# A graph layer with a mixture of experts: experts scatter finished rows to the output by node number

## The reference

```
logits = h @ gate_w + gate_b                      # h = layernorm(x), 3125 x 256; 8 experts
idx, prb = argmax(softmax(logits)), max(softmax(logits))
pos = rank of the token among those of its expert; kept = pos < C      # C = 489
buf[idx, pos] = h                                 # 8 x 489 x 256, empty slots are 0
ybuf = relu(buf @ w1 + b1) @ w2 + b2              # w1 256 x 1024, w2 1024 x 256 per expert
y = nan_to_num(ybuf[idx, pos] * (prb * kept), nan=0, posinf=1e4, neginf=-1e4)
out = x + y
```

## Time and profile before

| what | us |
|---|---|
| median of three runs | 1727.82 (1725.07 to 1732.25) |
| the profiled execution's own time | 1727.49 |
| its span | 1725.8 |
| TensorE busy | 1058.0 (61%) |
| VectorE busy | 972.2 (56%) |
| GpSimd busy | 538.4 (31%) |
| ScalarE busy | 432.9 (25%) |

### The profile page before, as it was taken

One profiled execution on the slowest core, in us unless ns is written; L12 is line 12 of the kernel. 1 busy time (PEld: TensorE's weight loads), 2 busy tenths in 40 slices (PEclk: granted clock), 3 DMA queues, 4 the chain that ended last, 5 costly groups with the idle time before them and its releaser, 6 DMA issues. The chain is left out here.

```text
span 1725.8 us, 20777 instructions
## 1 busy us (share of the span) xinstructions
PE 1058.0 (61%) x4059; PEld 687.7 (40%) x4060; DVE 972.2 (56%) x2394; ACT 432.9 (25%) x1253; POOL 538.4 (31%) x608
## 2 busy tenths in 40 slices
PE   0489483655666556565656655565668709999950
PEld 0255251433343333343334333343335605666630
DVE  5479865667666666667666666666777400000016
ACT  1222251322222222222222222222232402212111
POOL 1234425333334344343333444333300060000024
PEclk9999765777677677668776777667789558999985
DMA  4622404443444444444334444444300231323214
GB/s 142 112 92 65 125 14 122 117 119 111 112 124 125 115 133 130 121 124 122 111 111 122 130 131 131 125 117 129 99 1 0 73 107 51 126 94 128 87 39 122
DMA packets 86446, 179.36 MB, mean 104 GB/s; under 512 B 14979, under 2 KB 51909, under 8 KB 86413
## 3 DMA queue, kind: packets, MB, share of 16 engines
q0 software_dynamic: 39872, 117.67, 24.9%
q1 hardware_dynamic: 42125, 57.30, 10.5%
q10 hardware_dynamic: 4416, 4.01, 0.7%
HBM read 157.65 MB, written 21.63 MB: 104 GB/s over the span
## 5 line engine op out<-in xcount | busy, mean ns | idle before, releaser
L1099 PE MATMUL at_pa<-at_pv,at_hot 128*125 128x264 f32 x832 | 321.5, 532 | 229.3 <-DVE agg L973 160.3
L1099 PEld LDWEIGHTS at_pa<-at_pv,at_hot 128*125 128x125 f32 x832 | 193.3, 253 | 329.5 <-issue 256.9
L1042 PE MATMUL at_pq<-q,at_hotT 125*128 x1248 | 232.7, 330 | 79.5 <-DVE at_prod L981 56.9
L845 POOL DMA_INDIRECT slot<-kv_d,idx x192 | 183.5, 956 | 294.9 <-ACT idx L854 239.7
L845 POOL DMA_INDIRECT at_slot<-kv_d,idx x192 | 183.4, 955 | 289.7 <-ACT idx L854 236.9
L1042 PEld LDWEIGHTS at_pq<-q,at_hotT 125*128 125x128 bf16 x1248 | 142.5, 114 | 165.4 <-issue 112.0
L973 DVE TENSOR_TENSOR agg<-agg,at_pa 125x264 f32 x416 | 176.4, 424 | 33.5 <-remote 6.8
L1436 DVE TENSOR_TENSOR yb<-xp,b 128x256 f32<-128x256 f32 (+1 forms) x32 | 13.6, 425 | 269.5 <-PE xp L1467 269.5
L1016 DVE TENSOR_TENSOR at_pv<-at_slot,at_pp 128x528 f32<-128x528 f32 x104 | 71.8, 700 | 125.0 <-remote 91.8
L1016 DVE TENSOR_TENSOR at_pv<-slot,at_pp 128x528 f32<-128x528 f32 x104 | 71.7, 700 | 121.4 <-remote 87.0
L902 DVE TENSOR_REDUCE at_sc<-at_prod 128x16 f32<-128x512 f32 x208 | 139.2, 670 | 0.0
(11 more groups left out here) (295 smaller groups left out, 1408.4 us busy)
## 6 DMA issues: line engine op xcount, KB each, us to landing
slot<-in_w SPq DMA_DIRECT2D x16, 1024.0 KB, 7.5
at_locrow<-loc_d SPq DMA_DIRECT2D x26, 500.0 KB
slots_d<-slot SPq DMA_DIRECT2D x7, 512.0 KB
kv_d<-vst SPq DMA_DIRECT2D x25, 128.9 KB
base<-in_x SPq DMA_DIRECT2D x5, 625.0 KB
kv_d<-kst SPq DMA_DIRECT2D x25, 125.0 KB
slot<-kv_d,idx POOLq DMA_INDIRECT x192
at_slot<-kv_d,idx POOLq DMA_INDIRECT x192
```

Source lines behind the costliest of these rows:

```text
L845: pool.indirect_dma_start(slot[par][:, u, :], None, m.kv_d, bass.IndirectOffsetOnAxis(ap=m.idx[:, par, u:u + 1].bitcast(U32), axis=0)).the ...
L1042: mm = pe.matmul(pq[j % 2][:, (u % 2) * D:(u % 2 + 1) * D], hotT[:, u, :], at(m.q3, window)[:, part, :], start=(part == 0), stop=(part == 2))
L1099: mm = pe.matmul(pa[u % 4][:, 0:H * VW], hot[:, u % 8, :], pv[:, u % 4, :, :].rearrange("p h c -> p (h c)"), start=True, stop=True)
```

## The change

Each slot row gets two more columns (RW = 258): the token's probability (PRB) and its node number as an integer (NODE). The tile of h that is scattered, `m.hx`, has them beside h; empty slots have a node number beyond all nodes, written when the slot rows are zeroed. `attention_out` stores the residual twice while it is made, in five groups of five tiles each: to `x2_d` in DRAM and to `out`, both by SyncE. In `experts`, GpSimd gathers the residual of the rows of expert e+1 from `x2_d` by the node numbers that came with the rows (`xb`), VectorE scales, does the nan_to_num and adds the residual for each tile of 128 rows (eight operations), and GpSimd scatters the tile to `out` by node number. Both indirect DMAs check the index against N - 1 and skip rows beyond it. A token that doesn't fit keeps the residual that `attention_out` stored. Slot rows and weights have semaphores of their own (`ex_rows`, `ex_in`), SyncE issues the weights ahead of the rows, and TensorE waits for `down_read`, which VectorE gives after the first of its operations. `combine`, `y_d` and `slot_i` are gone, and so are two VectorE operations in `route`. In `linear_attention` two chains of handshakes count on one semaphore each where they had one per step; waits and work are the same. The core of the diff:

```diff
@@ -29,6 +29,9 @@
...
+RW = D + 2
+PRB, NODE = D, D + 1
+NOBODY = 1 << 20
...
@@ -396,7 +399,7 @@
...
-                sp.wait_ge(S.zero_made, 1)
+                sp.wait_ge(S.zero_made, 2)
...
@@ -414,7 +417,9 @@
...
-                pool.memset(zero[:], 0.0).then_inc(S.zero_made, 1)
+                empty = zero.rearrange("p (a d) -> p a d", a=4)
+                pool.memset(empty[:, :, 0:NODE], 0.0).then_inc(S.zero_made, 1)
+                pool.memset(empty[:, :, NODE:RW].bitcast(I32), NOBODY).then_inc(S.zero_made, 1)
...
@@ -1145,6 +1150,11 @@
...
+                for g in range(NT // LG):
+                    r = slice(g * LG, (g + 1) * LG)
+                    sp.wait_ge(S.x2_made, LG * (g + 1))
+                    sp.dma_start(m.x2_d.rearrange("(t p) d -> p t d", p=TT)[:, r, :], m.base[:, r, :]).then_inc(S.x2_stored, 16)
+                    sp.dma_start(out.rearrange("(t p) d -> p t d", p=TT)[:, r, :], m.base[:, r, :]).then_inc(S.out_stored, 16)
...
@@ -1178,7 +1188,7 @@
...
-                    dve.tensor_scalar(at(m.h, t), at(m.base, t), at(mean.rearrange("p (t o) -> p t o", o=1), t), at(var.rearrange("p (t o) -> p t o", o=1), t),
+                    dve.tensor_scalar(at(m.hx, t)[:, 0:D], at(m.base, t), at(mean.rearrange("p (t o) -> p t o", o=1), t), at(var.rearrange("p (t o) -> p t o", o=1), t),
...
@@ -1287,11 +1298,13 @@
...
+                pool.iota(m.hx[:, :, NODE].bitcast(I32), pattern=[[TT, NT]], base=0, channel_multiplier=1).then_inc(S.nodes_made, 1)
+                pool.wait_ge(S.nodes_made, 1)
...
-                                            m.h[:, t, :], None).then_inc(S.scattered, 16)
+                                            m.hx[:, t, :], None).then_inc(S.scattered, 16)
...
@@ -1325,9 +1338,6 @@
...
-                st.then(dve.tensor_copy(m.slot_i[:, :], slot[:, :]))
-                st.then(dve.tensor_tensor(m.prb[:, :], m.prb[:, :], kept[:, :], ALU.mult))
...
@@ -1365,10 +1375,15 @@
...
-        hb = [sb(f"hb_{i}", [128, MT, D]) for i in range(2)]
+        hb = [sb(f"hb_{i}", [128, MT, RW]) for i in range(2)]
         hm = sb("hm", [128, FC, 512])
-        yb = sb("yb", [128, MT, D])
+        yb = sb("yb", [128, 2, MT, D])
+        y = sb("y", [128, D])
+        fin = sb("y_fin", [128, D], I32)
+        lo = sb("y_lo", [128, D])
...
@@ -1389,16 +1404,17 @@
...
-                    sp.dma_start(hb[par][:, 0:MT - 1, :], m.slots[bass.ds(e * CAP, 128 * (MT - 1)), :].rearrange("(c p) d -> p c d", p=128)).then_inc(S.ex_in[par], 16)
-                    sp.dma_start(hb[par][0:sizes[-1], MT - 1, :], m.slots[bass.ds(e * CAP + 128 * (MT - 1), sizes[-1]), :]).then_inc(S.ex_in[par], 16)
+                    sp.dma_start(hb[par][:, 0:MT - 1, :], m.slots[bass.ds(e * CAP, 128 * (MT - 1)), :].rearrange("(c p) d -> p c d", p=128)).then_inc(S.ex_rows[par], 16)
+                    sp.dma_start(hb[par][0:sizes[-1], MT - 1, :], m.slots[bass.ds(e * CAP + 128 * (MT - 1), sizes[-1]), :]).then_inc(S.ex_rows[par], 16)
...
                         e = 2 * k + par
+                        sp.wait_ge(S.down_read, MT * (e - 1))
+                        expert_weights(sp, m, io, e, par)
                         sp.wait_ge(S.y_stored, 16 * MT * (e - 1))
                         rows_of(e, par)
-                        expert_weights(sp, m, io, e, par)
...
+                def node_of(par, i):
+                    return bass.IndirectOffsetOnAxis(ap=hb[par][0:sizes[i], i, NODE:RW].bitcast(U32), axis=0)
+
+                def residual(e, par):
+
+                    pool.wait_ge(S.ex_rows[par], 32 * (e // 2) + 32)
+                    wait(pool, S.y_ready, MT * (e - 1))
                     for i in range(MT):
-                        act.wait_ge(S.y_ready, MT * e + i + 1)
-                        act.dma_start(m.y_d[bass.ds(e * CAP + 128 * i, sizes[i]), :], yb[0:sizes[i], i, :]).then_inc(S.y_stored, 16)
-                rounds(act, body, True)
-                act.wait_ge(S.y_stored, 16 * MT * EX)
+                        pool.indirect_dma_start(xb[par][0:sizes[i], i, :], None, m.x2_d, node_of(par, i),
+                                                bounds_check=N - 1, oob_is_err=False).then_inc(S.base_in[par], 16)
+
+                def body(e, par):
+                    if e + 1 < EX:
+                        residual(e + 1, 1 - par)
+                    for i in range(MT):
+                        pool.wait_ge(S.y_ready, MT * e + i + 1)
+                        pool.indirect_dma_start(out, node_of(par, i), yb[0:sizes[i], par, i, :], None,
+                                                bounds_check=N - 1, oob_is_err=False).then_inc(S.y_stored, 16)
+                for x in xb:
+                    pool.memset(x[:], 0.0).then_inc(S.xb_made, 1)
+                pool.wait_ge(S.xb_made, 2)
+                pool.wait_ge(S.x2_stored, 16 * (NT // LG))
+                pool.wait_ge(S.out_stored, 16 * (NT // LG))
+                residual(0, 0)
+                for e in range(EX):
+                    body(e, e % 2)
+                pool.wait_ge(S.y_stored, 16 * MT * EX)
 
             @block.vector
             def _(dve):
-                def body(e, par, k):
-                    wait(dve, S.y_stored, 16 * MT * e)
+                st = m.dve_steps.on(dve)
+
+                def body(e, par):
+                    wait(dve, S.y_stored, 16 * MT * (e - 1))
                     for i in range(MT):
+                        rows = slice(0, sizes[i])
+                        v, f, l, h = y[rows, :], fin[rows, :], lo[rows, :], hi[rows, :]
+
                         dve.wait_ge(S.down_prod, MT * e + i + 1)
-                        dve.tensor_tensor(yb[0:sizes[i], i, :], p2[i % 2][0:sizes[i], 0:D], b2[par][0:sizes[i], :], ALU.add).then_inc(S.y_ready, 1)
-                rounds(dve, body)
+                        st.link(dve.tensor_tensor(v, p2[i % 2][rows, 0:D], b2[par][rows, :], ALU.add))
+                        dve.sem_inc(S.down_read, 1)
+                        st.link(dve.tensor_scalar(v, v, hb[par][rows, i, PRB:PRB + 1], None, ALU.mult))
+
+                        wait(dve, S.y_ready, MT * e + i)
+                        st.then(dve.tensor_scalar(f, v, 0.0, 0.0, ALU.mult, ALU.is_equal))
+                        st.then(dve.tensor_scalar(l, v, 0.0, -1.0e4, ALU.min, ALU.max))
+                        st.link(dve.tensor_scalar(h, v, 0.0, 1.0e4, ALU.max, ALU.min))
+                        st.link(dve.tensor_tensor(l, l, h, ALU.add))
+                        st.link(dve.copy_predicated(l, f, v))
+                        if i == 0:
+                            dve.wait_ge(S.base_in[par], 16 * MT * (e // 2 + 1))
+                        dve.tensor_tensor(yb[rows, par, i, :], l, xb[par][rows, i, :], ALU.add).then_inc(S.y_ready, 1)
+                for e in range(EX):
+                    body(e, e % 2)
 
...
@@ -1442,7 +1502,7 @@
...
-                    pe.wait_ge(S.ex_in[par], 80 * k + 80)
+                    pe.wait_ge(S.ex_rows[par], 32 * k + 32)
...
@@ -1451,6 +1511,7 @@
...
+                    pe.wait_ge(S.ex_in[par], 48 * k + 48)
...
@@ -1462,7 +1523,7 @@
...
-                        wait(pe, S.y_ready, MT * e + i - 1)
+                        wait(pe, S.down_read, MT * e + i - 1)
...
@@ -1471,87 +1532,14 @@
...
-def combine(nc, m, out):
...
```

More of the change, by code:

```diff
@@ L1109, in _, with attention_out @@
                 rounds(pe, body)
-def attention_out(nc, m, io):
+def attention_out(nc, m, io, out):
     with ExitStack() as ctx:
@@ L1270, in route @@
         L = m.logit
+        prb = m.hx[:, :, PRB]
         with nc.Block() as block:
@@ L1355, in expert_weights, with experts @@
     sp.dma_start(m.b2[par][:, :], io.b2[one, :].to_broadcast([128, D])).then_inc(m.sem.ex_in[par], 16)
-def experts(nc, m, io):
+def experts(nc, m, io, out):
     MT = -(-CAP // 128)
@@ L1367, in experts @@
         b1 = sb("b1", [128, EX, FC])
-        hb = [sb(f"hb_{i}", [128, MT, D]) for i in range(2)]
+        hb = [sb(f"hb_{i}", [128, MT, RW]) for i in range(2)]
+        xb = [sb(f"xb_{i}", [128, MT, D]) for i in range(2)]
         hT = [sb(f"hT_{i}", [128, 2, 512]) for i in range(2)]
         hm = sb("hm", [128, FC, 512])
-        yb = sb("yb", [128, MT, D])
+        yb = sb("yb", [128, 2, MT, D])
+        y = sb("y", [128, D])
+        fin = sb("y_fin", [128, D], I32)
+        lo = sb("y_lo", [128, D])
+        hi = sb("y_hi", [128, D])
         pt = [ctx.enter_context(nc.psum_tensor(f"xpt{i}", [128, 512], F32)) for i in range(2)]
@@ L1623, in graph_layer @@
     m.kv_d = dram("kv_d", (N, KV))
-    m.slots = dram("slots_d", (EX * CAP + N, D))
-    m.y_d = dram("y_d", (EX * CAP, D))
+    m.slots = dram("slots_d", (EX * CAP + N, RW))
+    m.x2_d = dram("x2_d", (N, D))
     with ExitStack() as ctx:
@@ L1690, in graph_layer @@
             m.b1n = att.enter_context(nc.sbuf_tensor("b1n", [EX * FF // 128, 128], F32))
-            m.h = m.q3.rearrange("p t a d -> p (t a d)")[:, 0:NT * 2 * D].bitcast(F32).rearrange("p (t d) -> p t d", t=NT)
```

(6 more changed lines are left out.)

134 lines of the change are left out of this document (38 added, 96 removed).

## The result

The changed kernel takes 1673.3 us (1670.5 to 1676.0, four runs) against 1728.4 (1725.1 to 1732.3, four runs) beside it: a ratio of 0.968, 95% interval 0.965 to 0.971. The forecast was 1668 us in a range of 1661 to 1688. The profiled execution took 1672.81 us with a span of 1671.1, which is 54.7 less than the 1725.8 before; 59.6 were forecast. The table splits the span where the prediction did.

A forecast was written before the change was run, and what follows sets the result against it. It took 62.7 us behind the last product, in `combine`, and TensorE in the experts as bounds: 1725.8 - 53.2 - 6.5 + 0.1 = 1666.2 us of span, plus 1.7 and 0.3 gives 1668 us; range 1661 to 1688.

The forecast's parts named there:

- The largest term: Behind the last product: all of `combine` goes, 62.7 us replaced by 9.5, so 53.2 us saved.
- The end: Last tile's own finish behind the last product: VectorE's operations, GpSimd's wake-up, issue, landing and block's end, 9.5 us.
- Chain: VectorE's eight operations on the last tile: 2.68 us plus five hand-overs at 0.04, together 2.88 us.
- Wake-up: GpSimd wakes after VectorE's last operation, before writing the scatter's descriptors: 0.38 us.
- landing and the block's end: After the last scatter's issue: 5.06 us, taken from the last slot scatter; bounds of the whole finish 7.6 to 14.2.
- The experts: Transposes' waits for a DMA in six of eight experts go; rows arrive at 1617.4 against 1619.12 needed: 6.5 us saved.
- Rival A: In the experts, scatters land late under weight traffic, so rows come late: 1677 to 1693 us, middle near 1683; chance 0.20.
- VectorE, GpSimd, the stores: VectorE's 2.88 us per tile, GpSimd's 11.9 us per expert and `attention_out`'s doubled stores stay hidden: no cost.
- rival D: GpSimd's queue in the expert loop becomes the bound; at 5.0 + 0.3 us a piece 97 us more, 1765 us; chance 0.04.
- Routing: Two VectorE operations go, 0.2 us saved; 25 scatters of 1032-byte rows cost 0.3 more: net +0.1 us.
- Rival B: In the experts, each 128-row scatter uses one engine, landing takes some 7.5 us: 1689 us; chance 0.04.
- Rival C: In the slot scatters, five engines are busy and wide unaligned rows slow them, 35.95 us become 45: 1677 us; chance 0.11.

The follow-up runs named there:

- e3: Kernel before, with slot rows and weights on two semaphores and transposes waiting for rows only, issue order unchanged: 1721.5 us, ratio 0.997 to the kernel before.
- e1: Changed kernel, with SyncE fetching slot rows ahead of the weights, both behind the stored outputs: 1673.35 us, ratio 0.969 to the kernel before.
- e5: Changed kernel without nan_to_num in the experts, five VectorE operations fewer per tile: 1461.4 us, ratio 0.963 to the kernel before.
- e6: Changed kernel with slot rows of 384 words (1536 bytes) instead of 258 (1032 bytes): 1478.4 us, ratio 0.972 to the kernel before.
- e4: Changed kernel with rows, then weights, issued together behind the stored outputs on one semaphore: 1714.3 us, ratio 0.993 to the kernel before.
- e7: Changed kernel without GpSimd's drains at the ends of the route and experts blocks, semaphore waits kept: 1458.3 us, ratio 0.959 to the kernel before.

## Why the prediction was right, and where its steps were off

The largest term held: `combine` went, and nothing took its place but the last tile's own finish. Of the span the forecast missed 4.9 us: 2.4 at the end, 2.1 in the experts, 0.4 ahead of them.

- **The end, forecast 9.5 us, measured 11.9.** Chain 3.28 for 2.88: 0.15 us pass between the first add and the multiply, where the semaphore is given, the multiply takes 0.35 instead of 0.28, and the first clip 0.44 instead of 0.21 to the next one's start. The first clip is slow wherever an indirect DMA instruction of GpSimd ends within it, as that of the tile before does here (1659.79, for 0.98); the multiply takes 0.35 with and without GpSimd. Wake-up 0.85 for 0.38, issue 0.98 for 1.19. The step that failed was "landing and the block's end", 5.06 us copied from the slot scatters. It was the sum of two things that don't scale together: a landing, and a drain that is 2.09 us long for 25 indirect DMAs and 5.27 for 64. For the last tile they are 1.1 and 5.27. The trace of before had both pieces; I read only their sum. Its answer on the block of `route`:

```profile
L1271 POOLq DRAIN  x1: 2083/2083/2083, 1420.7 to 1420.7; - x1
```

  With 1.1 and 5.27 in place of 5.06 the forecast of the end would have been 10.8.
- **The experts, forecast 6.5 us saved, measured 4.4 (2.4 us of waits left, 0.3 gained elsewhere).** That b2 held the transposes is confirmed by e3. The rows come 13.3 to 13.9 us behind the last add's start in the four experts that wait; the forecast had 11.4 (1606.04 to 1617.4), and TensorE asks at 13.1. The step that failed most is the landing: with GpSimd's instruction 1.19 + 2.87 = 4.1 us were forecast, and in the chain it was 4.9 to 5.3. I had argued that the weights would be on their way from 1607.0 and still took the landing of a quiet gather; e1 shows that it is 2.6 at most when the weights wait. Another 0.9 us are the chain (3.3 for 2.88) and the wake-up (0.87 for 0.38), as at the end, and e5 shows that a shorter chain removes the waits too. Rival A had the mechanism, a landing that takes longer under the weights, at 5.75 us behind the instruction and with 7 us of waits. The weights came at 388 GB/s, not 296, so the stretch in which they harm was shorter than I had it. The waits left are a third of rival A's 7 us, and the measured time lies between the forecast and A: they should have been one case with a sliding cost.
- **VectorE, GpSimd, the stores: forecast nothing, measured nothing.** VectorE waits 164 us for TensorE in the experts. GpSimd's 64 operations cost 1.0 us each, and 32 more cost little but their drain, so rival D falls: checking the bounds made no operation dear. The stores of `attention_out` end before the stage does.
- **Routing: forecast +0.1, measured +0.46.** The 25 scatters didn't grow. The rest is the second wait ahead of the first scatter, 0.7 us, which I had passed over because iota was early: a wait that is long fulfilled still costs when it shares its instruction with the one that counts.
- **Rival B (one engine per scatter)** falls: 128 rows into 3125 land in 2.5 us at the median, GpSimd's instruction included, where it needed 7.5 behind the instruction. (Of those, the 1.4 us of latency stand in no row.) The Trainium skill's rule ("DMA: Bandwidth & Descriptors", section "Why a DMA increments its semaphore by 16 and not by 1") does not decide here by the rows of the indexed target.
- **Rival C (wide rows)** falls, and with it the prediction's statement that five full engines set the scatters' pace: e6 passes 130 GB/s at the same pitch. The share of 0.32 was no limit of the scatters, only what GpSimd fed; rows of 1032 bytes cost nothing there (36.0 us for 24 steps with either).

`linear_attention` ends with such a drain as well, 2.30 us long, of which some 1.4 us lie behind GpSimd's last add (16 gathers); taking it away was not tried, since the first writes of the attention are ordered by it. What stays open: what decides when the clock comes up in expert 0's up products; what bounds the drain behind 400 gathers; why the attention runs 200 us faster on two of the three chips; and how much of the 1.4 to 2.3 us from fetching rows first arrives in the time.

## What to carry to other kernels

When a stage is removed, the price of its end has to be taken apart into the last transfer's landing and what the block itself does behind it; a drain of GpSimd's queue grew with the number of indirect DMAs up to the 96 tried here, and in these blocks it stood behind a semaphore wait that had already seen each of them land. A transfer that others wait for should be issued ahead of a large one on whose arrival nobody waits yet, or have the chain ahead of it shortened by as much. And a wait of some 3 us or more that is put on TensorE can cost half as much again by the clock that is lost with it (e4: 24.3 us of waits cost 37.1).

## What was not expected of the hardware

- The drain at a block's end: 46 ns, and 82 ns more for each indirect DMA that GpSimd has issued in the block (25: 2.09 us, 64: 5.27, 96: 7.89), on top of a wait that has seen every one land. With 400 gathers in the attention's block it is far less than that (6.0 us behind the last gather).
- From the start of GpSimd's instruction a scatter of 128 rows lands in 2.1 to 2.6 us when traffic is at 36 GB/s (e1), and in up to 6.0 under 388 GB/s of weights (7.5 once, in e7).
- After 3.3 to 5.4 us of waiting, 8 transposes take 1.8 to 1.9 us instead of 1.00 to 1.06; in the six turns of e4 the next 64 products take 14.7 to 16.1 us instead of 14.0.
- A VectorE clip of 128x256 takes 0.27 to 0.29 us, also when a GpSimd indirect DMA runs throughout it, and 0.38 to 0.55 when that instruction ends within it (17 of the 32 first clips in the changed kernel's trace).
- The kernel before takes 1728 us on one chip and 1522 on another; the gain of the change is 55 us on both.
